# Projected pieces from float32r parts, and values 17 columns wide, in a layer of two causal attentions and a routed network

## The chip, the cores and the metric

The kernel runs on one core of one Trainium2 chip. The metric is the device time of one execution in microseconds (us); the profiled execution also has a span, from its first to its last instruction. Engines are called as in the profile: PE (TensorE; PEld is its weight load), DVE (VectorE), ACT (ScalarE), POOL (GpSimd) and SP (SyncE, which issues the DMAs).

## The reference, cut to what matters

```python
B, T, C = x.shape                       # 32, 512, 256; 16 heads of 16 channels
q, k = split(x @ W_attn + b_attn)       # W_attn 256 x 512
y = causal_attn(q, k, v=x)              # softmax(q k^T / 4) v, per head
e = x[1:] - y[:-1]
k2 = x[:-1] @ W_k2 + b_k2               # W_k2 256 x 256
y2 = causal_attn(q[1:], k2, e)          # with a zero row ahead
a = y @ W_proj + b_proj + y2 @ W_proj + b_proj
x1 = layernorm(x + a)
out = layernorm(x1 + routed)            # routed: 8 experts, two a row, for the 512 rows of batch 0; zero for the rest
```

The router has indices for 512 rows only, those of batch 0. The kernel computes their routed network in the last stretch of its time; for the other batches the second normalization follows the first.

## The kernel before, in words

All five engines run one written-out schedule. Time is a counter: ten slots make a unit, eight units (places 0 to 7) make a batch; there are 32 batches. A unit is one group of four heads of one of the two attentions: places 0 to 3 are the four groups of the first attention, 4 to 7 those of the second. The engines meet by semaphores only, and each works its instructions strictly in the order of the program.

In each slot PE makes a bank of transposed scores (`score_t`, L631) for the unit of now, and a bank of scores (`score`, L642) for the unit five ahead, out of which DVE takes the row maxima (L824). Queries and keys lie in stacks of three float32r parts (high, high, low against high, low, high), so that one pass over 48 to 52 rows gives nearly a float32 product. ACT turns `score_t` into `prob` by exp (L500). There are two `score_t` banks, so PE's slot n waits for the exp of slot n - 2. After every odd slot POOL cuts the triangle of a pair (L422). PE multiplies `prob` by the values in slots 7, 1 and 3 (`weigh`, L592): four heads side by side, each in 32 of the array's columns, with `value[:, kb, head, :]` as stationary operand: 16 channels, a column of ones whose product is the sum of the weights, and 15 more columns of ones that nothing reads. ACT copies all of `out_t` in slot 3 (L524), and PE turns it in slot 5 (L674).

Six pieces a batch project x: `k0` at (place 7, slot 9), `q0` (0, 9), `k1` (1, 9), `q1` (2, 9), `k20` (4, 9), `k21` (5, 9). Each is two float32 products of 128 x 512 into `misc` (L696): the half c = 0 in slot 5, c = 1 in slot 9. A float32 product stands in the trace as two matmul instructions with two weight loads. ACT adds the bias (L518), POOL splits the piece into `part_h` and `part_l` three slots later (L442, L444), and SP copies the parts into the stacks. `x_t` (x turned by the host) has two buffers, loaded two batches ahead.

The normalization of a batch without the routed network is taken twice. The second one, for batches 1 on, lies in place 6 of the batch after: DVE takes statistics in slots 0 to 4, POOL adds epsilon at (6, 5) (`var_eps`, L471), ACT guesses the root at (6, 6) (L260, L262), POOL refines it at (6, 7) in six small operations that end in `shift` (`refine`, L243 to L255), and ACT applies it at (6, 9), (7, 1), (7, 3) and (7, 5) (L267). The first one lies at places 4 and 5 in the same manner.

```python
# POOL, in each time step, in this order:
#   affine_select of the pair (odd slots)   waits s_exp >= time + 1
#   bias add (2, 5); split of a piece, three slots after it
#   slot 0: value2 or y_sum; (4,7) (6,5): var_eps; (4,9) (6,7): refine
# ACT, in each time step:
#   exp; neg_h (7,1) (3,1); piece; slot 3: heads_t; guess_rstd (6,6); apply_norm (6,9) (7,1) (7,3) (7,5)
if now >= KEY_DEPTH:                     # PE, KEY_DEPTH = 2
    e.wait_ge(s_exp, now - KEY_DEPTH + 1)
```

Of the kernel before, what the change touches and what calls it, by code (L numbers as in the profile page):

```python
# [7 lines left out]
F32 = mybir.dt.float32  # L8
F32R = mybir.dt.float32r
# [5 lines left out]
P = 128  # L15
# [49 lines left out]
def build_layer(nc, x, x_turned, w_attn, b_qk, w_k2, w_proj, b_proj,  # L65
# [15 lines left out]
    with ctx:  # L81
# [6 lines left out]
        def sem(name):  # L88
# [3 lines left out]
        wq = sb("wq", [P, halves, 2 * halves, P])  # L92
        wk2 = sb("wk2", [P, halves, halves, P])
# [11 lines left out]
        value1 = sb("value1", [P, blocks, HEADS, 32])  # L105
        value2 = sb("value2", [P, blocks, HEADS, 32])
# [6 lines left out]
        x_t = [sb(f"x_t{i}", [P, halves, tokens]) for i in range(2)]  # L113
# [28 lines left out]
        s_x, s_xt = sem("s_x"), [sem(f"s_xt{i}") for i in range(2)]  # L142
# [3 lines left out]
        s_const, s_ones, s_bias = (sem(f"s_{n}") for n in ("const", "ones", "bias"))  # L146
# [10 lines left out]
        s_mask, s_split, s_value2, s_added, s_biased, s_ln = (  # L157
            sem(f"s_{n}") for n in ("mask", "split", "value2", "added", "biased", "ln"))
# [127 lines left out]
        def _(e):  # L286
            e.dma_start(x_t[0][:, :, :], x_turned[0].rearrange("(h p) t -> p h t", p=P)).then_inc(s_xt[0], 16)
            e.dma_start(wq[:, :, :, :], w_attn.rearrange("(h p) (w n) -> p h w n", p=P, n=P)).then_inc(s_weights, 16)
            e.dma_start(bias_qk[:, :], b_qk).then_inc(s_weights, 16)
            e.dma_start(wk2[:, :, :, :], w_k2.rearrange("(h p) (w n) -> p h w n", p=P, n=P)).then_inc(s_weights, 16)  # L290
# [8 lines left out]
            e.dma_start(x_t[1][:, :, :], x_turned[1].rearrange("(h p) t -> p h t", p=P)).then_inc(s_xt[1], 16)  # L299
# [4 lines left out]
            for time in times:  # L304
# [18 lines left out]
                if (place, slot) == (0, 8) and 2 <= b < batches:  # L323
                    e.wait_ge(s_piece, N_PIECES * (b - 1))
                    e.dma_start(x_t[b % 2][:, :, :], x_turned[b].rearrange("(h p) t -> p h t", p=P)).then_inc(s_xt[b % 2], 16)
# [69 lines left out]
        def _(e):  # L395
# [16 lines left out]
            for time in times:  # L412
# [22 lines left out]
                if piece:  # L435
                    n, i = piece[3], piece[3] % 2
                    e.wait_ge(s_full, n + 1)
                    if n >= 2:

                        was, was_hf = [v[:2] for v in PIECES.values() if v[2] == (n - 2) % N_PIECES][0]  # L440
                        e.wait_ge(s_stack[was, was_hf], 16 * TERMS * SIDES * ((n - 2) // N_PIECES + 1))
                    e.tensor_copy(part_h[i][:, :], part_f[i][:, :]).then_inc(s_split, 1)  # L442
                    e.wait_ge(s_split, 2 * n + 1)
                    e.tensor_tensor(part_l[i][:, :], part_f[i][:, :], part_h[i][:, :].bitcast(F32), ALU.subtract).then_inc(s_split, 1)  # L444

# [133 lines left out]
        def _(e):  # L579
            e.wait_ge(s_const, 11)  # L580

            def weigh(unit, kb, first, count, start=False, stop=False):
# [12 lines left out]

            for time in times:
# [81 lines left out]
                for c in range(halves):  # L678
                    piece = piece_ending(place, slot + 4 * (1 - c), ahead, batches)
                    if piece:  # L680
                        kind, hf, b, n = piece
                        if c == 0:
                            if n == 0:
                                e.wait_ge(s_weights, WEIGHTS)
                            if n % N_PIECES == 0:
                                e.wait_ge(s_xt[b % 2], 16 * (b // 2 + 1))
# [302 lines left out]
```

## Time and profile before

| | |
|---|---|
| median of 3 runs | 2663.38 us (2663.15 to 2669.7) |
| the profiled execution, its time | 2670.42 us |
| its span | 2668.7 us |
| PE busy, DVE, ACT, POOL | 94%, 81%, 69%, 54% |
| mean granted clock of TensorE | 0.976 |

The profiled execution is 7.0 us above the median, and 1.7 us of its time lie outside the span. Busy PE is time in which a matmul is in flight; records of following matmuls overlap, so what a matmul costs is read from the distance between starts or from the chain, not from its duration.

### The profile page before, as it was taken

Reading aid. Unit: us, or ns where it says so; the run is one execution under the profiler, and the core shown is the slowest. Engines: PE = TensorE matmul, PEld = TensorE weight load, DVE = VectorE, ACT = ScalarE, POOL = GpSimd, SP = SyncE. Lnnn points to the kernel's source line nnn. Section 1 sums busy time; section 2 is a strip of 40 time slices with the busy share of each in tenths; the row PEclk is TensorE's granted clock in tenths of the full one; section 3 lists DMA queues with packets and bytes.
Section 4 is the critical chain, followed back from the end, with each engine's and each line's share of the span. In section 5 each row is a group of like instructions: output and inputs, shape, how many; then the busy total and the mean of one; then the engine's idle time right before and its main releaser. Section 6 shows DMA issues by size and latency. Waiting matters only on the chain.

```text
span 2668.7 us, 65100 instructions
## 1 busy us (share of the span) xinstructions
PE 2506.2 (94%) x19286; PEld 1227.1 (46%) x19286; DVE 2166.4 (81%) x9640; ACT 1831.6 (69%) x3574; POOL 1441.9 (54%) x2431
## 2 busy tenths in 40 slices
PE   3999999999999999999999999999999999999897
PEld 1444444444444444444444444444444444444454
DVE  2788888788888888888888888888888888888655
ACT  0477777677777776777777777777777777777653
POOL 2355556556555555655555555555555555555432
PEclk8799999999999999999999999999999999999998
DMA  5455545465555555655455555554555654455211
GB/s 95 87 104 94 93 79 105 91 113 102 104 93 88 93 102 102 113 101 96 91 85 103 99 109 105 105 94 91 86 102 101 114 101 94 87 86 93 63 52 51
DMA packets 187784, 251.23 MB, mean 94 GB/s; under 512 B 26768, under 2 KB 103192, under 8 KB 187416
## 3 DMA queue, kind: packets, MB, share of 16 engines
q1 hardware_dynamic: 187440, 247.07, 50.5%
q8 instruction: 164, 2.69, 0.5%
q14 instruction: 180, 1.47, 0.3%
HBM read 74.60 MB, written 16.78 MB: 34 GB/s over the span
## 4 chain that ended last, share of the span: by engine, by line
PE 77%; DVE 7%; issue 6%; ACT 5%; POOL 3%; SPq 1%; DMA 1%; ACTq 0%; POOLq 0%; DVEq 0%
PE score_t L631 22%; PE out_t L592 21%; PE misc L696 13%; PE score L642 9%; PE misc L731 4%; DVE junk L824 4%; PE turn L674 4%; ACT prob L500 3%; PE score L779 2%; ACT y_t L532 1%; PE misc L718 1%; PE score L795 1%; POOL prob L422 1%; DVE resid L875 1%; DVE max_cols L824 1%
## 5 line engine op out<-in xcount | busy, mean ns | idle before, releaser
L824 DVE CUSTOM_DVE_ANT_0 junk<-score,mask_rows 128x384 bf16<-128x384 f32 (+3 forms) x3584 | 1692.9, 514 | 387.6 <-PE score L642 385.8
L500 ACT ACTIVATE prob<-score_t 128x512 f32<-128x512 f32 x2560 | 1401.5, 596 | 578.3 <-PE score_t L631 573.5
L422 POOL TENSOR_SCALAR_AFFINE_SELECT prob<-prob 128x512 f32<-128x512 f32 (+1 forms) x1280 | 725.9, 568 | 1038.8 <-ACT prob L500 1038.8
L631 PE MATMUL score_t<-stack_q,stack_k 50*128 50x128 f32 (+5 forms) x4096 | 1060.2, 365 | 72.5 <-ACT prob L500 47.6
L642 PE MATMUL score<-stack_k,stack_q 48*128 48x512 f32 (+3 forms) x4096 | 1047.9, 354 | 8.0 <-DMA stack_q<-part_l 5.9
L631 PEld LDWEIGHTS score_t<-stack_q,stack_k 50*128 50x128 f32 (+1 forms) x4096 | 604.1, 186 | 812.7 <-ACT prob L500 689.1
L592 PE MATMUL out_t<-prob,value 128*32 128x512 f32 (+3 forms) x8192 | 719.3, 446 | 0.0
L642 PEld LDWEIGHTS score<-stack_k,stack_q 48*128 48x128 f32 x4096 | 610.8, 189 | 25.4 <-DVE max_cols L824 16.0
L696 PE MATMUL misc<-x_t,wq 128*128 128x512 f32 x512 | 289.5, 650 | 60.9 <-DMA bias<-L_attn_b_proj 31.7
L824 DVE DVE_READ_ACCUMULATOR2_ANT max_cols<- 128x1 f32 x4096 | 338.1, 83 | 0.0
L592 PEld LDWEIGHTS out_t<-prob,value 128*32 128x32 f32 x8192 | 189.0, 109 | 317.2 <-issue 216.0
L444 POOL TENSOR_TENSOR part_l<-part_f,part_h 128x512 fp32r<-128x512 f32 x192 | 245.5, 1279 | 16.4
L518 ACT ACTIVATE part_f<-misc,bias_qk 128x512 f32<-128x512 f32 x192 | 131.9, 687 | 106.1 <-PE misc L696 101.4
L267 ACT ACTIVATE resid<-resid,shift,rstd 128x256 f32<-128x256 f32 x248 | 149.0, 603 | 47.6 <-POOL shift L255 47.6
L674 PE MATMUL turn<-ident,heads_t 128*128 128x128 f32 x1024 | 169.2, 288 | 0.0
L524 ACT ACTIVATE heads_t<-out_t 128x512 f32<-128x512 f32 x256 | 154.2, 602 | 2.2 <-PE out_t L592 2.0
L442 POOL CAST part_h<-part_f 128x512 fp32r<-128x512 f32 x192 | 117.8, 614 | 63.2 <-ACT part_f L518 54.6
L824 DVE CUSTOM_DVE_ANT_0 junk<-score,mask_first 128x128 bf16<-128x128 f32 x512 | 146.3, 286 | 0.0
L696 PE MATMUL misc<-x_t,wk 128*128 128x512 f32 x256 | 141.5, 635 | 0.0
L674 PEld LDWEIGHTS turn<-ident,heads_t 128*128 128x128 f32 x1024 | 108.6, 141 | 47.4 <-ACT heads_t L524 25.3
L731 PE MATMUL misc<-wp,y_t 128*128 128x256 f32 x512 | 127.4, 392 | 0.0
L696 PEld LDWEIGHTS misc<-x_t,wq 128*128 128x128 f32 x512 | 79.6, 195 | 98.9 <-issue 75.4
(83 smaller groups left out, 1380.9 us busy)
## 6 DMA issues: line engine op xcount, KB each, us to landing
stack_k<-part_h SPq DMA_DIRECT2D x512, 128.0 KB, 4.2
stack_k<-part_l SPq DMA_DIRECT2D x256, 128.0 KB, 4.5
stack_q<-part_h SPq DMA_DIRECT2D x256, 128.0 KB, 4.2
x_t<-x_turned SPq DMA_DIRECT2D x32, 512.0 KB, 9.6
x_in<-L_attn_x SPq DMA_DIRECT2D x32, 512.0 KB, 13.4
stack_q<-part_l SPq DMA_DIRECT2D x128, 128.0 KB, 5.1
resid<-L_attn_x SPq DMA_DIRECT2D x32, 512.0 KB, 6.3
layer_out<-resid SPq DMA_DIRECT2D x31, 512.0 KB, 11.6
```

The lines of the kernel that those rows point to most:

```text
L267: e.activation(dst[:, t, :], src[:, t, :], ACT.Identity, bias=shift[:, t:t + 1], scale=rstd[:, 4, t:t + 1]).then_inc(s_apply, 1)
L422: e.affine_select(out=view, in_=view, compare_op=ALU.is_ge, fill=0.0, base=-unit_parts(unit)[1], pattern=[[0, runs], [0, cut], [1, P]], ch ...
L444: e.tensor_tensor(part_l[i][:, :], part_f[i][:, :], part_h[i][:, :].bitcast(F32), ALU.subtract).then_inc(s_split, 1)
L500: e.activation(prob[pair % RING][:, slot % 2 * 512:slot % 2 * 512 + 512], score_t[time % KEY_DEPTH][:, :], ACT.Exp, scale=1.0 / np.sqrt(HE ...
L524: e.activation(heads_t[:, :], out_t[:, :], ACT.Copy).then_inc(s_heads, 1)
L592: done = e.matmul(out_t[32 * h:32 * h + 32, first:first + count], value[:, kb, GROUP * g + h, :], prob[pair % RING][:, at:at + count], sta ...
L631: done = e.matmul(score_t[now % KEY_DEPTH][:, col:col + n], keys[rows, pair, kb * P:(kb + 1) * P], stack_q[b % 2][rows, pair, kb * P:token ...
L642: done = e.matmul(score[number % MAX_DEPTH][:, col:col + n], stack_q[b % 2][rows, pair, qb * P:(qb + 1) * P], keys[rows, pair, 0:n], start ...
L674: done = e.transpose(turn[:, t * P:(t + 1) * P], heads_t[:, t * P:(t + 1) * P], ident[:, :])
L696: done = e.matmul(misc[:, :], w, x_t[b % 2][:, c, :], start=(c == 0), stop=(c == halves - 1))
L731: done = e.matmul(misc[:, j * width:(j + 1) * width], y_t[:, c, t * P:(t + 1) * P], wp[:, c, :], start=(c == 0), stop=(c == halves - 1))
L824: e.tensor_tensor_reduce(junk[count % JUNK][:, 0:n], score[number % MAX_DEPTH][:, col:col + n], mask, 1.0, -3e38, ALU.add, ALU.max, max_co ...
```

## The change

Three things change together. The projections read float32r parts of x turned (`x_t[HIGH]`, `x_t[LOW]`) and of the weights, and do high x high, low weight x high x, and high weight x low x: three one-pass products in place of each float32 one. The weights are split once at the start by DVE; x turned is loaded into one full buffer, `x_full`, and split by POOL at (6, 4) and (6, 7), ahead of the batch's first piece. The values keep 17 of their 32 columns; `out_t` is cleared once, since the rows between the heads are no longer written. The load of x turned for a batch moves behind the split of the batch before it.

```diff
-        wq = sb("wq", [P, halves, 2 * halves, P])
-        wk2 = sb("wk2", [P, halves, halves, P])
+        wq = [sb(f"wq_{part}", [P, halves, 2 * halves, P], F32R) for part in "hl"]
+        wk2 = [sb(f"wk2_{part}", [P, halves, halves, P], F32R) for part in "hl"]
...
-        value1 = sb("value1", [P, blocks, HEADS, 32])
-        value2 = sb("value2", [P, blocks, HEADS, 32])
+        value1 = sb("value1", [P, blocks, HEADS, HEAD_DIM + 1])
+        value2 = sb("value2", [P, blocks, HEADS, HEAD_DIM + 1])
...
# SP
-            e.dma_start(x_t[1][:, :, :], x_turned[1].rearrange("(h p) t -> p h t", p=P)).then_inc(s_xt[1], 16)
...
-                if (place, slot) == (0, 8) and 2 <= b < batches:
-                    e.wait_ge(s_piece, N_PIECES * (b - 1))
-                    e.dma_start(x_t[b % 2][:, :, :], x_turned[b].rearrange("(h p) t -> p h t", p=P)).then_inc(s_xt[b % 2], 16)
+                if (place, slot) == (0, 8) and 1 <= b < batches:
+                    e.wait_ge(s_xsplit, 2 * halves * b)
+                    e.dma_start(x_full[:, :, :], x_turned[b].rearrange("(h p) t -> p h t", p=P)).then_inc(s_xt, 16)
...
# POOL, behind the split of a piece and ahead of slot 0's work, var_eps and refine
+                for c in range(halves):
+                    b = ahead + 2
+                    if (place, slot) == (6, (4, 7)[c]) and 0 <= b < batches:
+                        if c == 0:
+                            e.wait_ge(s_xt, 16 * (b + 1))
+                            if b:
+                                e.wait_ge(s_piece, N_PIECES * b)
+                        e.tensor_copy(x_t[HIGH][:, c, :], x_full[:, c, :]).then_inc(s_xsplit, 1)
+                        e.wait_ge(s_xsplit, 2 * (halves * b + c) + 1)
+                        e.tensor_tensor(x_t[LOW][:, c, :], x_full[:, c, :], x_t[HIGH][:, c, :].bitcast(F32),
+                                        ALU.subtract).then_inc(s_xsplit, 1)
...
# PE
-                    done = e.matmul(out_t[32 * h:32 * h + 32, first:first + count], value[:, kb, GROUP * g + h, :],
+                    done = e.matmul(out_t[32 * h:32 * h + HEAD_DIM + 1, first:first + count], value[:, kb, GROUP * g + h, :],
...
-                        w = wk2[:, c, hf, :] if kind == "k2" else wq[:, c, hf + (0 if kind == "q" else halves), :]
-                        done = e.matmul(misc[:, :], w, x_t[b % 2][:, c, :], start=(c == 0), stop=(c == halves - 1))
+                        for i, (pw, px) in enumerate(zip(PARTS_K, PARTS_Q)):
+                            w = wk2[pw][:, c, hf, :] if kind == "k2" else wq[pw][:, c, hf + (0 if kind == "q" else halves), :]
+                            done = e.matmul(misc[:, :], w, x_t[px][:, c, :], start=(c == 0 and i == 0),
+                                            stop=(c == halves - 1 and i == TERMS - 1))
...
# DVE, at the start
+            e.memset(out_t[:, :], 0.0).then_inc(s_ones, 1)
...
             e.wait_ge(s_weights, WEIGHTS)
+            for i, (parts, full) in enumerate(((wq, wq_full), (wk2, wk2_full))):
+                e.tensor_copy(parts[HIGH][:, :, :, :], full[:, :, :, :]).then_inc(s_wsplit, 1)
+                e.wait_ge(s_wsplit, 2 * i + 1)
+                e.tensor_tensor(parts[LOW][:, :, :, :], full[:, :, :, :], parts[HIGH][:, :, :, :].bitcast(F32),
+                                ALU.subtract).then_inc(s_wsplit, 1)
```

## Rows read from the trace of the kernel before

**Rows 1.** The page, its first part: busy time and share of the span.

```profile
PE 2506.2 (94%) x19286; PEld 1227.1 (46%) x19286; DVE 2166.4 (81%) x9640; ACT 1831.6 (69%) x3574; POOL 1441.9 (54%) x2431
```

**Rows 2.** Weight loads by shape: count, busy us, mean ns, idle before.

```profile
L592 PEld LDWEIGHTS out_t<-prob,value 128*32 128x32 f32 x8192 | 189.0, 109 | 317.2 <-issue 216.0 <-POOL prob L422 100.4
...
L696 PEld LDWEIGHTS misc<-x_t,wq 128*128 128x128 f32 x512 | 79.6, 195 | 98.9 <-issue 75.4 <-ACT part_f L518 7.0
```

**Rows 3.** What PE waited for, 100 to 2500 us: total, times, longest.

```profile
PE score_t L631 <- ACT prob L500: 46.3, 67, 1.0
```

**Rows 4.** Busy time by unit of one batch (window, length, PE, PEld, DVE, ACT, POOL).

```profile
1366.88:1376.57 9.69, 9.14 (x75) 4.12 (x73) 9.42 (x44) 6.89 (x16) 5.46 (x13) 1.00 0.01 3
sum 76.61, PE 73.42 PEld 35.84 DVE 65.32 ACT 56.02 POOL 44.19; mean PE 9.18 PEld 4.48 DVE 8.17 ACT 7.00 POOL 5.52
```

**Rows 5.** The chain that ended last: start, length, what.

```profile
1300.62 0.86 PE misc L696 x2
...
1303.92 1.05 PE misc L696 x2
...
1305.68 1.01 PE out_t L592 x16
```

**Rows 6.** Timeline, PE, one-pass products of 512 columns on the same 64 rows.

```profile
1306.63 0.72 PE L642 MATMUL score<-stack_k,stack_q 48*128 48x512 f32 x2
...
1306.97 0.40 PE L631 MATMUL score_t<-stack_q,stack_k 52*128 52x512 f32 x1
```

**Rows 7.** Timeline, POOL, from slot 2 of place 6.

```profile
1307.14 0.61 POOL L442 CAST part_h<-part_f 128x512 fp32r<-128x512 f32 x1
1307.83 1.28 POOL L444 TENSOR_TENSOR part_l<-part_f,part_h 128x512 fp32r<-128x512 f32 x1
1309.06 0.43 POOL L422 TENSOR_SCALAR_AFFINE_SELECT prob<-prob 128x256 f32<-128x256 f32 x1
...
1310.56 0.23 POOL L471 TENSOR_SCALAR var_eps<-mean_var 128x4 f32<-128x4 f32 x1
1311.82 0.64 POOL L422 TENSOR_SCALAR_AFFINE_SELECT prob<-prob 128x512 f32<-128x512 f32 x1 [1.03 <-ACT prob L500]
...
1313.83 0.23 POOL L255 TENSOR_SCALAR shift<-log_var 128x4 f32<-128x4 f32 x1
```

**Rows 8.** Timeline, ACT, the same stretch.

```profile
1310.82 0.21 ACT L260 ACTIVATE log_var<-var_eps 128x4 f32<-128x4 f32 x1
...
1311.17 0.58 ACT L500 ACTIVATE prob<-score_t 128x512 f32<-128x512 f32 x1
...
1314.09 0.60 ACT L267 ACTIVATE resid<-resid,shift,rstd 128x256 f32<-128x256 f32 x1 [0.65 <-POOL shift L255]
1314.59 1.06 ACT L500 ACTIVATE prob<-score_t 128x512 f32<-128x512 f32 x2
1315.97 0.27 ACT L509 ACTIVATE neg_h<-turn 64x128 fp32r<-64x128 f32 x1 [0.32 <-PE turn L705]
...
1317.59 0.59 ACT L524 ACTIVATE heads_t<-out_t 128x512 f32<-128x512 f32 x1
```

**Rows 9.** Timeline, PE, slots 2 and 5 of place 7.

```profile
1315.87 0.49 PE L631 MATMUL score_t<-stack_q,stack_k 52*128 52x512 f32 x1
...
1318.23 0.66 PE L674 MATMUL turn<-ident,heads_t 128*128 128x128 f32 x4
```

**Rows 10.** Timeline, PE, a long wait near the end of the span.

```profile
2616.61 2.44 PE L795 MATMUL score<-down_w,inner 128*128 128x256 f32 x8 [2.32 <-DVE ffn L934]
```

**Rows 11.** Windows around it; third number from the end: PE's granted clock.

```profile
2618.00:2620.00 2.00, 2.00 (x5) 1.30 (x4) 0.88 (x3) 1.26 (x2) 0.59 (x1) 0.50 0.00 0
2620.00:2622.00 2.00, 2.00 (x4) 0.73 (x4) 0.69 (x1) 0.00 (x0) 0.67 (x1) 0.64 0.48 131
```

**Rows 12.** Timeline, PE, the first piece.

```profile
31.68 3.75 PE L696 MATMUL misc<-x_t,wq 128*128 128x512 f32 x4 [31.68 <-DMA bias<-L_attn_b_proj]
```

**Rows 13.** Timeline, DVE, one copy from SBUF to SBUF.

```profile
1374.94 0.71 DVE L832 COPY value<-x_in 128x1024 f32<-128x1024 f32 x1
```

More of the change, by code:

```diff
@@ L104, in build_layer @@
         ones = nc.alloc_sbuf_tensor_at("ones", [2 * MAX_PARTS, pairs, tokens], F32R, offset=prob_at)
-        value1 = sb("value1", [P, blocks, HEADS, 32])
-        value2 = sb("value2", [P, blocks, HEADS, 32])
+        wq_full = nc.alloc_sbuf_tensor_at("wq_full", [P, halves, 2 * halves, P], F32, offset=prob_at + 4 * pairs * tokens)
+        wk2_full = nc.alloc_sbuf_tensor_at("wk2_full", [P, halves, halves, P], F32, offset=prob_at + 5 * pairs * tokens)
+        value1 = sb("value1", [P, blocks, HEADS, HEAD_DIM + 1])
+        value2 = sb("value2", [P, blocks, HEADS, HEAD_DIM + 1])
         x_in = sb("x_in", [P, blocks, width])
@@ L112, in build_layer @@
         y_t = sb("y_t", [P, halves, tokens])
-        x_t = [sb(f"x_t{i}", [P, halves, tokens]) for i in range(2)]
+        x_full = sb("x_full", [P, halves, tokens])
+        x_t = [sb(f"x_t_{part}", [P, halves, tokens], F32R) for part in "hl"]
         heads_t = sb("heads_t", [P, tokens])
@@ L141, in build_layer @@
         s_weights, s_rows, s_next, s_resid, s_out = (sem(f"s_{n}") for n in ("weights", "rows", "next", "resid", "out"))
-        s_x, s_xt = sem("s_x"), [sem(f"s_xt{i}") for i in range(2)]
+        s_x, s_xt = sem("s_x"), sem("s_xt")
         s_stack = {(kind, hf): sem(f"s_stack_{kind}{hf}") for kind in ("q", "k", "k2") for hf in range(halves)}
         s_maxrow = [sem(f"s_maxrow{i}") for i in range(2)]
-        s_const, s_ones, s_bias = (sem(f"s_{n}") for n in ("const", "ones", "bias"))
+        s_const, s_ones, s_bias, s_wsplit = (sem(f"s_{n}") for n in ("const", "ones", "bias", "wsplit"))
         s_key, s_qry, s_pv, s_turned, s_piece, s_yt_pe, s_proj, s_neg_pe = (
@@ L155, in build_layer @@
             sem(f"s_{n}") for n in ("max", "negl", "value1", "den", "rden", "normal", "attended", "stats", "aggr"))
-        s_mask, s_split, s_value2, s_added, s_biased, s_ln = (
-            sem(f"s_{n}") for n in ("mask", "split", "value2", "added", "biased", "ln"))
+        s_mask, s_split, s_xsplit, s_value2, s_added, s_biased, s_ln = (
+            sem(f"s_{n}") for n in ("mask", "split", "xsplit", "value2", "added", "biased", "ln"))
         s_fin, s_fbias = sem("s_fin"), sem("s_fbias")
@@ L286, in _ @@
         def _(e):
-            e.dma_start(x_t[0][:, :, :], x_turned[0].rearrange("(h p) t -> p h t", p=P)).then_inc(s_xt[0], 16)
-            e.dma_start(wq[:, :, :, :], w_attn.rearrange("(h p) (w n) -> p h w n", p=P, n=P)).then_inc(s_weights, 16)
+            e.dma_start(x_full[:, :, :], x_turned[0].rearrange("(h p) t -> p h t", p=P)).then_inc(s_xt, 16)
+            e.dma_start(wq_full[:, :, :, :], w_attn.rearrange("(h p) (w n) -> p h w n", p=P, n=P)).then_inc(s_weights, 16)
             e.dma_start(bias_qk[:, :], b_qk).then_inc(s_weights, 16)
-            e.dma_start(wk2[:, :, :, :], w_k2.rearrange("(h p) (w n) -> p h w n", p=P, n=P)).then_inc(s_weights, 16)
+            e.dma_start(wk2_full[:, :, :, :], w_k2.rearrange("(h p) (w n) -> p h w n", p=P, n=P)).then_inc(s_weights, 16)
             R, M = SCORE_ROWS, MAX_PARTS
@@ L580, in _ @@
             e.wait_ge(s_const, 11)
+            e.wait_ge(s_ones, 3)
             def weigh(unit, kb, first, count, start=False, stop=False):
@@ L684, in _ @@
                                 e.wait_ge(s_weights, WEIGHTS)
+                                e.wait_ge(s_wsplit, 4)
                             if n % N_PIECES == 0:
-                                e.wait_ge(s_xt[b % 2], 16 * (b // 2 + 1))
+                                e.wait_ge(s_xsplit, 2 * halves * (b + 1))
                             if n:
```

## Prediction

> **What bounds the kernel now.** I read the page first: PE is busy for 94% of the span, DVE for 81%, the others less [rows 1]. A busy PE need not be the bound, so next came the view by unit of one batch in the steady part, 1299.96 to 1376.57 us, cut where PE turns the heads (slot 5): the batch takes 76.6 us, and PE has a matmul in flight in 73.4 of them, DVE works 65.3 [rows 4]. The waits of PE say the same: from 100 to 2500 us it waited 46 us for ACT's exp, in 67 waits of at most 1.0 us [rows 3]. So PE's stream sets the time, and what is taken out of it is gained, where nobody else is close behind. DVE is close in one unit, from slot 5 of place 4 on, with 9.42 of 9.69 us [rows 4]. The last view was the timeline of places 6 and 7, for POOL, ACT and PE [rows 7 to 9]: there the batch's second normalization makes a chain over DVE, POOL and ACT, and ACT's exp, which PE needs two slots later, stands behind it.
>
> **The products.** A float32 product of 512 columns is two instructions. On the chain they take 0.86 us in slot 5 and 1.05 in slot 9 [rows 5]; the 0.19 more in slot 9, where PE comes from products on 64 rows, is the first weight load and the drain, and stays. 0.86 us over 512 columns is four passes of 0.213. For a float32r product over 128 rows there is no row. The nearest is that over 48 and 52 rows: behind the score product begun at 1306.63, with its weight load, the next on the same 64 rows begins 0.34 us later [rows 6], which leaves one pass of 0.21 beside a load of 0.11 to 0.13. So three products take three passes, 0.64, and each pair saves 0.21 us. The loads of the second and third lie under the pass before. Bounds: no less than three passes; no more than two passes for each product, six in all, 0.43 us more than now. I take one, the row shows it. There are 32 x 6 x 2 = 384 such pairs. Those in slot 9 of place 4 (32) save nothing, since PE then waits for DVE, full in that unit; that in slot 5 of place 4 does, as the exps of its unit and with them the first normalization come earlier by as much. The two of place 5 count too: the POOL chain below begins behind the exps and the piece of place 5. 352 x 0.213 = 75 us.
>
> **The values.** The weight load of 32 columns takes 109 ns, that of 128 takes 195 [rows 2]: 0.9 ns a column, 13 ns for 15 columns. Three groups of products a unit, 768 in all, each with one load ahead that nothing covers (four heads load side by side; later ones lie under passes). 768 x 13 ns = 10 us; below, nothing. I take 7, as some groups lie where PE has room. The passes don't change: their length is the columns of `prob`. The rest of what a group pays beyond streaming, 1.01 us less four passes of 0.213, is 0.16 us [rows 5].
>
> **POOL's new work, a wait that appears.** Each batch POOL gets two casts and two subtractions of 128 x 512, the shapes of the split of a piece. There the subtraction begins 0.69 us after the cast, and the next operation 1.23 after that [rows 7]: 1.92 us for a half. On POOL alone, 54% busy, that costs nothing. But it works in order, and behind the first half stand the triangle of slot 5 and `var_eps`, behind the second `refine`. Followed through place 6:
>
> - After the triangle of slot 3 (1309.06, 0.4 us to the next start) the first half runs from 1309.45 to 1311.37. The triangle of slot 5 takes 0.65 more, so `var_eps` begins at 1312.0, not 1310.56: 1.45 late [rows 7].
> - ACT's guess stands in program order ahead of the exp of slot 7, so that exp begins at 1312.6, not 1311.17 [rows 8].
> - The triangle of slot 7 goes from 1311.82 to 1313.27; then the second half, 1.92; then `refine`. `shift` now begins 2.01 after the triangle of slot 7, and will at 1313.27 + 1.92 + 2.01 = 1317.2, 3.37 late [rows 7].
> - ACT's first application waits for it: 1314.09 becomes 1317.46, and the exps of place 7's slots 0 and 1 behind it begin at 1317.96, not 1314.59 [rows 8]. PE's slot 2 waits for the first of them: 1318.5, not 1315.87 [rows 9].
> - ACT gets back the 0.32 us that it waited ahead of `neg_h` [rows 8], so from there it is 3.05 late, with no other gap up to the heads' copy in slot 3: 1317.59 becomes 1320.64, and PE's turn in slot 5 goes from 1318.23 to 1321.28 [rows 8, 9].
>
> From there PE has its own stream to work off, and 3.05 us are lost for good. Both bounds: 3.4 if ACT gets nothing back, 2.5 if PE's slot 2 alone is what is late. What else stands behind: on POOL the triangle of slot 9, wanted in slot 3 of place 7, where PE is late as well; `neg_h` and its DMAs, late with everything else. It happens where a batch has both the second normalization (from batch 1 on) and a later x to split (up to batch 31): in 28 rounds. 28 x 3.05 = 85 us.
>
> **What the stall does to PE's clock.** From about 1315.9 (the end of the weighing and a turn) to 1318.5 PE then does nothing, 2.6 us, and little in the 3 us before. In the steady part the clock is 1.00 with waits of at most 1.0 us [rows 3, 4]. Near the end PE waited 2.32 us [rows 10], and 1.4 us after that wait the clock fell to 0.50, for 2 us and for 0.72 of the next window (at 0.64 in the mean): 3.4 us at 1.2 GHz [rows 11]. Such a stretch does 1.7 us less work; some 0.4 of it lies where PE waits for ACT anyway. So 1.3 us each time. Bounds: never, or after each of 28 stalls (36 us). I take three of five, as the new wait is a little longer than the one that was followed by a fall: 28 x 0.6 x 1.3 = 22 us.
>
> **The start.** DVE splits 1024 and 512 columns of weights ahead of the first piece. A copy of 1024 columns takes 0.71 us [rows 13]; by bounds of once and twice that for the larger cast and subtraction and half for the smaller, 2.1 to 4.3 us, I take 3.1. The first piece, at half clock, took 3.75 us for two float32 products, eight passes of 0.43 and a load [rows 12]; with six single passes of 0.43 it takes 2.6, and two pieces lie ahead of the first scores: 2.2 less. One 512 KB load leaves the start: about 1 less. Together nothing.
>
> **The sum.** 85 - 75 - 7 + 0 + 22 = 25 us more, against the profiled execution's 2670.4 us (span 2668.7, 1.7 around it): 2695. That execution was 7.0 above the median, so against 2663.4 I say 2688.
>
> **One rule weighed.** By the Trainium skill, "TensorE: Matmul & The Clock Gate", section "Weight-path perf modes", weights of 128 columns whose type is not float32 load by a faster way, measured there at about twice the speed. The float32r loads of this trace are of 128 columns, and their load in the 0.34 us of [rows 6] shows none of it. By the rule each product group in slot 9 would save half of its first load of about 0.11 us, 192 x 0.055 = 11 us; by the row, nothing, and the sum goes by the row.
>
> **The rivals.**
> 1. *The stall without the clock's fall.* For it: PE still does some work in the 3 us before the gap. Then 25 - 22 = 3 us more: 2666, between 2652 and 2678.
> 2. *The narrow values pay for more than a load (the other side).* If all of the 0.16 us that a group costs beyond its passes goes by the width of the weights, 15/32 of it, 0.075 us, is saved in each of 768 groups: 58 us instead of 7. With the stall and no fall of the clock: 2666 - 51 = 2615; with the fall 2637. It decides from 21 ns a group on (16 us, twice the bound for a change that shows). Against it: most of that 0.16 should be the way through the array and its drain, which have nothing to do with width.
> 3. *The products load faster.* If a float32r load of 128 columns takes 0.055 us less than the 0.11 of [rows 6], the 192 groups in slot 9 save 11 us: 2677. This is what the rule above would do here.
> 4. *A float32r product over 128 rows is two passes.* 352 x 0.64 = 225 us more than in the sum: 2913. Against it: [rows 6].
> 5. *The clock stays down for longer after each stall.* If two such stretches follow each stall, 28 x 2 x 1.5 = 84 in place of 22: 2750.
>
> **How the numbers follow.** My forecast (stall and fall) 0.45, with its own range 2674 to 2704; rival 1 0.23; rival 2 0.15; rival 3 0.06; rival 4 0.02; rival 5 0.09. What a measurement can tell from no change is 0.3%, 8 us: 2655 to 2671. Slower: all of the forecast but little, rivals 3 to 5, a quarter of rival 1: 0.63. The same: most of rival 1: 0.17. Faster: rival 2 and the low end of rival 1: 0.20. The range 2630 to 2718 leaves out rivals 4 and 5 and the lower half of rival 2, under 2 in 10.
>
> **What would show it.** Right: ACT's wait for `shift` in place 6 of about 3.3 us where it is 0.65 now; PE's waits for the exp up by some 70 to 90 us; in the chain more POOL and ACT; product groups of three at 0.64 us in slot 5; windows at 0.5 clock behind the stalls. Wrong: no new wait of ACT; three products over 0.7 us; value groups shorter by more than 0.03 us; a batch period away from the places' stall that shrinks by less than 2 us. The prediction fails most easily in the balance of two terms near 80 us, in which an error of 10% in one is the 0.3% that can be told.

## The result, and the profile after

The changed kernel takes 2752.24 us (median of 4 runs, 2748.9 to 2754.43) against 2663.27: 1.0328 times as long, with an interval of 1.0307 to 1.0349. I had forecast 2688, slower, with a range that ends at 2718. The direction was right, the size was not: 89 us in place of 25.

The page of the changed kernel, the line that answers to [rows 1]:

```profile
PE 2524.4 (92%) x19670; PEld 1323.2 (48%) x19670; DVE 2174.3 (79%) x9645; ACT 1829.0 (66%) x3574; POOL 1557.0 (57%) x2559
```

PE is busy for 18 us more, and its share falls. So the time did not go into PE's work alone: waits came in. The waits of the changed kernel, 100 to 2600 us (total, times, longest), to be set beside [rows 3]:

```profile
ACT resid L270 <- POOL shift L258: 110.1, 58, 3.1
PE score_t L647 <- ACT prob L515: 109.1, 127, 2.5
ACT log_var L263 <- POOL var_eps L486: 41.1, 28, 1.7
```

The last row is the count that the prediction needed: 28 rounds in which ACT waits for `var_eps`. PE's wait for the exp is 63 us above the 46.3 of [rows 3], which end at 2500 us. One round, POOL's timeline (start, length, what; it answers to [rows 7]):

```profile
1349.37 0.41 POOL L424 TENSOR_SCALAR_AFFINE_SELECT prob<-prob 128x256 f32<-128x256 f32 x1
1349.74 0.60 POOL L456 CAST x_t_h<-x_full 128x512 fp32r<-128x512 f32 x1
1350.43 1.28 POOL L458 TENSOR_TENSOR x_t_l<-x_full,x_t_h 128x512 fp32r<-128x512 f32 x1
...
1352.38 0.23 POOL L486 TENSOR_SCALAR var_eps<-mean_var 128x4 f32<-128x4 f32 x1
1353.64 0.64 POOL L424 TENSOR_SCALAR_AFFINE_SELECT prob<-prob 128x512 f32<-128x512 f32 x1 [1.03 <-ACT prob L515]
1354.23 0.61 POOL L456 CAST x_t_h<-x_full 128x512 fp32r<-128x512 f32 x1
1354.93 1.29 POOL L458 TENSOR_TENSOR x_t_l<-x_full,x_t_h 128x512 fp32r<-128x512 f32 x1
...
1357.59 0.23 POOL L258 TENSOR_SCALAR shift<-log_var 128x4 f32<-128x4 f32 x1
```

From the triangle of slot 7 (1353.64) to `shift` (1357.59) it is 3.95 us; in [rows 7] it was 2.01. ACT in the same stretch (it answers to [rows 8]), then PE (to [rows 9]):

```profile
1352.64 0.20 ACT L263 ACTIVATE log_var<-var_eps 128x4 f32<-128x4 f32 x1 [1.68 <-POOL var_eps L486]
...
1357.85 0.60 ACT L270 ACTIVATE resid<-resid,shift,rstd 128x256 f32<-128x256 f32 x1 [3.09 <-POOL shift L258]
1358.36 1.06 ACT L515 ACTIVATE prob<-score_t 128x512 f32<-128x512 f32 x2
```

```profile
1356.22 0.30 PE L724 MATMUL turn<-ident,max_cols 128*64 128x128 f32 x1
1358.98 0.50 PE L647 MATMUL score_t<-stack_q,stack_k 52*128 52x512 f32 x1 [2.46 <-ACT prob L515]
...
1362.46 1.12 PE L690 MATMUL turn<-ident,heads_t 128*128 128x128 f32 x4
```

The rows show the chain of the prediction: `shift` late, the exp behind it late, PE idle for 2.46 us. The last row belongs to the term that I had undersized. The turn of four blocks takes 1.12 us where [rows 9] has 0.66: PE now works at 1.2 GHz. Windows over the same stretch (third number from the end: the granted clock):

```profile
1356.00:1358.00 2.00, 0.52 (x13) 0.12 (x3) 0.27 (x2) 0.15 (x1) 1.58 (x8) 1.00 0.03 3
1358.00:1360.00 2.00, 1.02 (x4) 0.39 (x4) 0.45 (x1) 2.00 (x6) 1.52 (x3) 0.90 0.00 0
1360.00:1362.00 2.00, 2.00 (x17) 1.06 (x16) 1.05 (x5) 1.79 (x5) 0.41 (x1) 0.50 0.04 8
1362.00:1364.00 2.00, 2.00 (x10) 1.57 (x9) 1.49 (x8) 1.78 (x4) 0.64 (x1) 0.50 0.14 29
1364.00:1366.00 2.00, 2.00 (x11) 1.17 (x9) 0.24 (x1) 0.21 (x1) 0.01 (x1) 0.50 0.45 94
1366.00:1368.00 2.00, 2.00 (x20) 0.78 (x17) 1.93 (x12) 1.03 (x3) 0.64 (x1) 0.89 0.35 119
```

The clock is down for 6.8 us here. By windows of 1 us over the whole span, the changed kernel has 28 stretches at half clock between 300 and 2520 us, one in each of the 28 rounds: 20 of 6.8 us, 7 of 10.2 and one of 3.4, 212 us together. The kernel before has nine in the same part of the span, 41 us, each 1.0 to 2.2 us behind a wait of 1.0 us for the exp.

A round of the changed kernel has two waits of PE: one of 0.9 us, which the kernel before has as well (1.0 there), and about 5 us later the long one. In 21 rounds the fall comes in the long wait or at most 2.1 us after it, as above. In the 7 rounds with 10.2 us it comes before the long wait, 1.2 to 2.5 us behind the short one, and lasts through the long one, of which 1.2 to 2.3 us are left, as PE, slow by then, comes to it later. One of these rounds, PE's two waits and one window between them:

```profile
951.83 0.38 PE L647 MATMUL score_t<-stack_q,stack_k 52*128 52x256 f32 x1 [0.89 <-ACT prob L515]
...
957.18 0.79 PE L647 MATMUL score_t<-stack_q,stack_k 52*128 52x512 f32 x1 [1.47 <-ACT prob L515]
```

```profile
954.00:955.00 1.00, 1.00 (x16) 0.34 (x8) 0.66 (x4) 0.00 (x0) 0.83 (x4) 0.50 0.33 41
```

The products and values, in the chain of waits that ended last (they answer to [rows 5]) and in the weight loads (to [rows 2]; count, busy us, mean ns):

```profile
1373.33 0.70 PE misc L714 x3
...
1376.45 0.89 PE misc L714 x3
...
1378.23 0.99 PE out_t L608 x16
```

```profile
L608 PEld LDWEIGHTS out_t<-prob,value 128*17 128x17 f32 x8192 | 163.3, 97 | 317.2 <-issue 197.2 <-POOL prob L424 119.7
...
L714 PEld LDWEIGHTS misc<-x_t_h,wq_h 128*128 128x128 f32 x256 | 53.2, 208 | 96.4 <-issue 75.1 <-ACT part_f L533 4.5
```

Three float32r products take 0.70 us in slot 5 and 0.89 in slot 9, against 0.86 and 1.05: 0.16 less, not 0.21. The group over the values takes 0.99 for 1.01.

### The profile page after: what moved, and what is told of

The parts are those of the page before. It is cut to its first block, busy times and chain, and to the rows that moved or that the text cites. A ratio compares the mean times of both kernels' runs of the same rounds, so it can differ in the third digit from the quotient of the medians.

```text
span 2752.2 us, 66033 instructions
## 1 busy us (share of the span) xinstructions
PE 2524.4 (92%) x19670; PEld 1323.2 (48%) x19670; DVE 2174.3 (79%) x9645; ACT 1829.0 (66%) x3574; POOL 1557.0 (57%) x2559
## 4 chain that ended last, share of the span: by engine, by line
PE 63%; POOL 13%; ACT 10%; issue 9%; DVE 4%; SPq 1%; DMA 1%; ACTq 0%; POOLq 0%; DVEq 0%
PE score_t L647 18%; PE out_t L608 16%; PE misc L714 10%; PE score L658 7%; ACT prob L515 6%; PE misc L750 4%; POOL prob L424 4%; PE turn L690 3%; POOL x_t_l L458 3%; DVE junk L849 2%; PE score L798 1%; ACT y_t L547 1%; PE misc L737 1%; ACT resid L270 1%; POOL x_t_h L456 1%
## 5 line engine op out<-in xcount | busy, mean ns | idle before, releaser
L647 PE MATMUL score_t<-stack_q,stack_k 50*128 50x128 f32 (+5 forms) x4096 | 1116.6, 377 | 131.2 <-ACT prob L515 109.4
L658 PE MATMUL score<-stack_k,stack_q 48*128 48x512 f32 (+3 forms) x4096 | 1101.4, 364 | 11.5 <-DMA stack_q<-part_l 9.4
L647 PEld LDWEIGHTS score_t<-stack_q,stack_k 50*128 50x128 f32 (+1 forms) x4096 | 634.8, 192 | 781.9 <-ACT prob L515 611.5
L608 PE MATMUL out_t<-prob,value 128*17 128x512 f32 (+3 forms) x8192 | 723.3, 449 | 0.0
L658 PEld LDWEIGHTS score<-stack_k,stack_q 48*128 48x128 f32 x4096 | 641.8, 194 | 24.2 <-DVE max_cols L849 12.6
L608 PEld LDWEIGHTS out_t<-prob,value 128*17 128x17 f32 x8192 | 163.3, 97 | 317.2 <-issue 197.2
L714 PE MATMUL misc<-x_t_h,wq_h 128*128 128x512 f32 x256 | 135.5, 529 | 63.9 <-DVE wk_l L830 34.6
L444 POOL CAST part_h<-part_f 128x512 fp32r<-128x512 f32 x192 | 131.1, 683 | 62.8 <-ACT part_f L533 51.9
L714 PE MATMUL misc<-x_t_l,wq_h 128*128 128x512 f32 x256 | 110.0, 430 | 0.0
L714 PE MATMUL misc<-x_t_h,wq_l 128*128 128x512 f32 x256 | 109.6, 428 | 0.0
```

The costliest lines, as they stand in the source:

```text
L608: done = e.matmul(out_t[32 * h:32 * h + HEAD_DIM + 1, first:first + count], value[:, kb, GROUP * g + h, :], prob[pair % RING][:, at:at + c ...
L647: done = e.matmul(score_t[now % KEY_DEPTH][:, col:col + n], keys[rows, pair, kb * P:(kb + 1) * P], stack_q[b % 2][rows, pair, kb * P:token ...
L658: done = e.matmul(score[number % MAX_DEPTH][:, col:col + n], stack_q[b % 2][rows, pair, qb * P:(qb + 1) * P], keys[rows, pair, 0:n], start ...
L714: done = e.matmul(misc[:, :], w, x_t[px][:, c, :], start=(c == 0 and i == 0), stop=(c == halves - 1 and i == TERMS - 1))
```

## The experiments

The runs are compared by their times and by one table from the traces: the time from one turn of the heads (slot 5) to the next, in us by place, as a median over the 28 batches that have a stall in the changed kernel. "1-2" is the time from the turn in place 1 to that in place 2, "6-0" that from place 6 to place 0 of the next batch. The last column is the time at half clock between 120 and 2600 us. None of it is a single row: it is worked out from the starts of the four-block turns and from the granted clock. The kernel before was timed again beside each series of runs and took 2663.3 to 2666.9 us, so a difference between two series carries some 3 us.

```
kernel                  1-2    2-4    4-5    5-6    6-0    0-1    batch   half clock
before                  9.90   20.59  9.72   8.88   18.27  9.25   76.61    51
values only             9.85   20.56  9.71   8.86   18.26  9.22   76.46    65
behind normalization    9.53   20.26  9.55   8.71   18.09  9.07   75.21    31
wait filled             9.53   20.26  9.51   8.71   21.01  9.07   78.09    48
after                   9.54   20.24  9.53   8.71   23.37  9.07   80.46   212
first half only         9.53   20.25  9.57   8.71   19.37  9.07   76.50    85
splits alone            9.85   20.56  9.68   8.86   23.73  9.21   81.89   283
six in slot 5          10.23   20.95 10.24   9.42   19.88  9.77   80.49    96
one product             9.07   21.72  9.46   8.39   17.78  8.59   75.01    82
one product, late bias  9.08   19.78  9.46   8.39   17.78  8.59   73.08   112
```

**Values only.** The kernel before with nothing but the values 17 wide:

```diff
-        value1 = sb("value1", [P, blocks, HEADS, 32])
-        value2 = sb("value2", [P, blocks, HEADS, 32])
+        value1 = sb("value1", [P, blocks, HEADS, HEAD_DIM + 1])
+        value2 = sb("value2", [P, blocks, HEADS, HEAD_DIM + 1])
...
-                    done = e.matmul(out_t[32 * h:32 * h + 32, first:first + count], value[:, kb, GROUP * g + h, :],
+                    done = e.matmul(out_t[32 * h:32 * h + HEAD_DIM + 1, first:first + count], value[:, kb, GROUP * g + h, :],
```

> The kernel before with only the values cut to 17 columns (and the one clearing of out_t that goes with it); projections, x and weights as before. If the narrow weight load is worth what its 12 ns say (97 against 109 ns, 768 groups), the time falls by up to 9 us: 2654 to 2663. If the narrow values are part of the 89 us, through another way of loading or a slower product, it rises by 20 us or more. If the whole fixed part of a group went by the width, it falls to about 2615.

Measured: 2667.11 us against 2666.86, ratio 0.9997 (0.9984 to 1.001). By the table a batch is 0.15 us shorter, 5 us in all, and the time doesn't show even that. My second rival, that narrow values pay for more than a load, is out.

**No splits in the steady part.** The changed kernel, where GpSimd splits only the first x:

```diff
-                    if (place, slot) == (6, (4, 7)[c]) and 0 <= b < batches:
+                    if (place, slot) == (6, (4, 7)[c]) and b == 0:
```

> The changed kernel in which POOL splits x for batch 0 only; the later splits are left out, so every batch is projected from batch 0's x. Theory A (POOL's splits delay the second normalization, and all of the loss is the stall behind it and the halved clock after it): the rest of the change is a gain, 2663 - 75 - 7 = about 2580, 2565 to 2600, and no episodes of half clock beyond those of the kernel before. Rival B (the products, the values or the loads cost time themselves): 2640 or more.

Measured: 2619.56 us, ratio 0.9818 (0.9802 to 0.9834). The stall and its clock are worth 133 us (2752.24 less 2619.56), but the gain left is 47 us, not 82: the products save less than I had said. This was the first sign of an error on each side of the sum.

**The wait filled.** The changed kernel with nine products of 512 columns on PE inside the wait, written to a bank that is overwritten later. The stall of everybody else stays; only PE's idleness goes:

```diff
+                if (place, slot) == (7, 1) and 2 <= ahead <= batches - 3:
+                    for _ in range(FILL):
+                        e.matmul(misc[:, :], wq[HIGH][:, 0, 0, :], x_t[HIGH][:, 0, :], start=True, stop=True)
```

> The changed kernel with nine products of 128x512 put on PE into the wait at slot 1 of place 7, of batches that split x; nobody reads their output, and they fit in the 2.5 us in which PE waits for the exp. Theory A1 (what costs most is not the wait but the clock that is halved after it, 6.8 us in most batches): the stalls stay and the time falls by 60 to 80 us, to 2675 to 2695, and the mean granted clock goes back from 0.947 to 0.97 or more. Rival A2 (the wait costs by itself, the clock is a mark of it only): 2752 within 10 us, or more by the added work.

Measured: 2701.82 us, ratio 1.0127 (1.0108 to 1.0146), 50 us less than the changed kernel, with 9 x 28 products more. PE's timeline in one round, and the windows around it:

```profile
1331.81 2.33 PE L730 MATMUL misc<-x_t_h,wq_h 128*128 128x512 f32 x9
...
1334.49 0.50 PE L648 MATMUL score_t<-stack_q,stack_k 52*128 52x512 f32 x1 [0.34 <-ACT prob L516]
```

```profile
1335.00:1337.00 2.00, 1.93 (x18) 0.89 (x18) 1.78 (x6) 2.00 (x6) 0.81 (x2) 1.00 0.04 8
1337.00:1339.00 2.00, 2.00 (x18) 1.47 (x15) 1.24 (x9) 1.96 (x6) 0.48 (x1) 1.00 0.09 21
```

The score product still waits for its exp, and in this round the clock behind it stays at 2.4 GHz. No round has a fall behind the filled wait. In 13 of the 28 the clock falls ahead of it all the same, 1.3 to 2.2 us behind the short wait of 0.9 us, and for 3.4 us each time. Summed over all batches, the way from place 6 to 0 is 82 us longer than without the stall (the next run), and in the changed kernel, where the long wait is empty, a further 55. The times say the same: 84 us for the stall (2701.82 less 2618.27), 50 for the clock (2752.24 less 2701.82). The 84 still hold a few us of clock, 48 us at half against 31. The 50 us belong to 164 us more at half clock: one us at half clock costs about a third of a us here.

**The splits behind the normalization.** The changed kernel with the two halves at place 6, slot 7, behind `refine`, and place 7, slot 2; each half of a piece's products waits for its own half of x:

```diff
-                    if (place, slot) == (6, (4, 7)[c]) and 0 <= b < batches:
+                    if (place, slot) == ((6, 7), (7, 2))[c] and 0 <= b < batches:
```

> The changed kernel with the same splits of x, but issued on POOL behind the normalization: the first half after refine at (6, 7), the second at (7, 2), and each product waits for its half only. All work is kept. Theory A: the place of the splits and not their amount costs the time; ACT's wait for shift goes back to about 0.7 us, and the time is near that of the kernel without splits, 2575 to 2605. Rival C (POOL has no room for 3.8 us more a batch wherever they lie, since the triangles behind them come late): 2640 or more.

Measured: 2618.27 us, ratio 0.9817 (0.9798 to 0.9836). It leaves nothing out, and it is faster than both kernels, by 1.8% than the one before: the work on POOL costs nothing that shows once nothing urgent stands behind it. Its waits, 100 to 2600 us:

```profile
ACT resid L270 <- POOL shift L258: 45.9, 59, 2.8
PE score_t L648 <- ACT prob L516: 43.3, 69, 1.0
```

Both are back at about what they were ([rows 3]). The time is that of the run without splits, within 1.3 us. What I had expected, some 2580, was missed by the same 38 us in both, which is the products' term.

**One half in the way.** The changed kernel with the first half left at place 6, slot 4, and the second at place 7, slot 2:

```diff
-                    if (place, slot) == (6, (4, 7)[c]) and 0 <= b < batches:
+                    if (place, slot) == ((6, 4), (7, 2))[c] and 0 <= b < batches:
```

> The changed kernel with the first half of the split where the change puts it (place 6, slot 4) and only the second moved behind the normalization (place 7, slot 2). GpSimd then reaches var_eps some 1.4 us late and the shift as much, instead of 1.45 and 3.37. Theory, that a stall costs what it lasts beyond some 0.3 us of cover and that the clock falls only behind a long one: 28 x 1.1 = 31 us above 2618, 2650 us, and fewer than ten stretches at half clock in the steady part. Rival, that every stall at this place brings a stretch at half clock: 31 + 50 = 81 us above, 2700 us, with a stretch behind each of the 28.

Measured: 2659.72 us, ratio 0.9976 (0.9958 to 0.9994), 41 us above the version behind the normalization; both of my figures, 31 and 81, miss it, the first by less. The waits:

```profile
ACT resid L270 <- POOL shift L258: 56.9, 58, 1.2
ACT log_var L263 <- POOL var_eps L486: 41.3, 29, 1.7
```

In the rounds without half clock the way from place 6 to 0 is 0.94 us longer (19.03 for 18.09), 26 us for 28 rounds; over all rounds it is 39 us longer. From 300 us on there are 17 stretches at half clock where the version behind the normalization has 6, 54 us more. So the short stall costs its length and sometimes the clock; only the rounds with the long one have a fall every time.

**The splits alone.** The kernel before with the values 17 wide, float32 products as ever, and GpSimd's four operations at the places of the change, written to tiles that nobody reads:

```diff
+                    if (place, slot) == (6, (4, 7)[c]) and 1 <= b < batches:
...
+                        e.tensor_copy(spare_h[:, :], x_t[b % 2][:, c, :]).then_inc(s_spare, 1)
+                        e.wait_ge(s_spare, k + 1)
+                        e.tensor_tensor(spare_l[:, :], x_t[b % 2][:, c, :], spare_h[:, :].bitcast(F32),
+                                        ALU.subtract).then_inc(s_spare, 1)
```

> The kernel before with the values 17 wide, and GpSimd's four split operations of the change at place 6, slots 4 and 7, for batches 1 to 29, written to spare tiles that nobody reads; the products stay full float32 ones. Theory, that the stall and the clock behind it belong to the place of the splits and have nothing to do with the products: 29 x 3 us of stall and some 50 us of clock on 2667, 2800 us, and a stretch at half clock behind each. Rival, that the clock's fall needs the float32r products (a TensorE that had been less busy before the wait): 2751 us, with few such stretches.

Measured: 2799.15 us, ratio 1.0514 (1.0499 to 1.053), with a stretch at half clock in each of the 28 rounds, here of 10.2 us in 27 of them. These 27 don't stand behind the long wait: they begin ahead of it, 1.3 to 1.9 us behind the short wait, which is mostly 1.06 us here, and last through it. PE's short wait in one round, and the window in which the clock is down first:

```profile
1293.16 0.38 PE L648 MATMUL score_t<-stack_q,stack_k 52*128 52x256 f32 x1 [1.06 <-ACT prob L516]
```

```profile
1295.00:1296.00 1.00, 1.00 (x12) 0.24 (x8) 0.96 (x4) 0.00 (x0) 0.92 (x3) 0.50 0.73 84
```

The splits cost 132 us on top of the values-only kernel, and the changed kernel has 134 on top of its version without the stall. So the loss doesn't need the float32r products, and the two parts of the change add up. Where in the round the clock falls, and for how long, isn't the same in the two kernels; why isn't shown.

**Six products in slot 5.** The version behind the normalization, with the three products of slot 5 done twice, the first time as a closed group whose result is overwritten:

```diff
-                        for i, (pw, px) in enumerate(zip(PARTS_K, PARTS_Q)):
+                        for extra, i, pw, px in [(more, i, *part) for more in ((True, False) if c == 0 else (False,))
+                                                 for i, part in enumerate(zip(PARTS_K, PARTS_Q))]:
```

> The kernel with the splits behind the normalization (2618.27 us), with the three products of slot 5 done twice (the first time as a closed group of their own, whose result is overwritten): 192 more trios, nothing else. If three float32r passes cost 3 x 0.23 = 0.69 us on the path, 132 us more, 2750 us; if they cost what I took in the prediction, 3 x 0.213 = 0.64, 123 us more, 2741 us. If half of it vanishes in waits that PE has anyway for exponentials or for VectorE, 2684 us; this would say that the saving of the products was lost in the same way.

Measured: 2765.83 us, ratio 1.0367 (1.0328 to 1.0406), 148 us more. Away from the clock each of the six trios of a batch takes 0.69 to 0.71 (9.53 to 10.23, 20.26 to 20.95, and so on; in place 6 to 0 the rounds without half clock take 18.8): 4.2 us a batch, 135 us. In the chain:

```profile
1301.99 1.41 PE misc L718 x6
...
1305.82 0.90 PE misc L718 x3
```

So a pass of 512 float32r columns is 0.235 us, and in slot 5 all of it lies on the path that sets the time. The other 13 us fit the clock (65 us more at half), and the four runs of this kernel lie between 2750 and 2775.

**One product.** The version behind the normalization with two of the three terms left out:

```diff
-                        for i, (pw, px) in enumerate(zip(PARTS_K, PARTS_Q)):
+                        for i, (pw, px) in enumerate([(HIGH, HIGH)]):
```

> The kernel with the splits behind the normalization (2618.27 us), each group of three float32r products cut to its first, high part times high part: two of the three terms of a projected piece are left out. 768 products of 512 columns go, of 0.23 us each by the pitch in the trace: 177 us of TensorE. Theory, that TensorE's own time sets the end in slot 5 but that in slot 9 the next group of scores waits for an exponential anyway: the 384 in slot 5 give 88 us, those in slot 9 between nothing and half of theirs, so 2480 to 2530 us, and the waits of PE for ACT grow. Rival, that TensorE is the bound everywhere: 2441 us. Rival, that VectorE's and ScalarE's waits take it all: 2600 us or more.

Measured: 2625.33 us, ratio 0.9877 (0.9838 to 0.9916). 177 us of PE's work taken out, and the kernel is 7 us slower than with it. It looks like proof that PE isn't the bound. The table says otherwise: every place got shorter but those from 2 to 4, which got 1.5 us longer in the median and 1.9 in the mean. POOL and then PE in place 2:

```profile
1324.45 0.64 POOL L424 TENSOR_SCALAR_AFFINE_SELECT prob<-prob 128x512 f32<-128x512 f32 x1 [1.29 <-ACT prob L516]
1328.26 2.35 POOL L432 TENSOR_TENSOR resid<-resid,bias 128x1024 f32<-128x1024 f32 x1 [3.17 <-DMA resid<-L_attn_x]
1330.56 1.27 POOL L424 TENSOR_SCALAR_AFFINE_SELECT prob<-prob 128x512 f32<-128x512 f32 x2
```

```profile
1331.25 1.66 PE L609 MATMUL out_t<-prob,value 128*17 128x384 f32 x12 [1.99 <-POOL prob L424]
```

With a faster PE, POOL comes to its bias add before the residual's load has landed, waits 3.17 us with two triangles behind it, and PE waits for those. This is the rule and no single case: from 100 to 2600 us POOL waits for that load 28 times, 67 us in all, and PE 27 times for such triangles, 36 us.

**One product, the bias add later.** The same with that add moved from place 2, slot 5 to slot 9:

```diff
-                if (place, slot) == (2, 5) and 0 <= ahead - 1 < batches:
+                if (place, slot) == (2, 9) and 0 <= ahead - 1 < batches:
```

> The kernel with one product for three (2625.33 us; two of three terms left out), with GpSimd's bias add to the second residual moved from place 2, slot 5 to slot 9 of the same place, so that it no longer waits 3.2 us for its load in front of a mask. Theory: that wait hid the worth of the products. By the turns of the trace the places away from it were 0.46 us shorter (two) or 0.32 (two), so with it gone a batch is some 2.6 us shorter than with three products: 2618 less 80 to 90 us, 2530 to 2545 us. Rival: the wait only took slack that was there, TensorE isn't what bounds the batch, and the time stays above 2600.

Measured: 2567.5 us, ratio 0.9629 (0.9602 to 0.9656). The stall is gone (19.78 in place of 21.72), and 58 us with it. A batch is 2.13 us shorter than with three products: 0.45 to 0.48 in 1-2, 2-4 and 0-1, 0.32 in 5-6, 0.31 in 6-0, 0.09 in 4-5. Of twelve groups that lost two passes, the equal of about four and a half shows. That is 68 us over the batches; 51 were measured. The clock takes the rest as far as it can be told (112 us at half, 31 with three products). Where the other seven and a half groups go isn't shown; PE's waits for DVE's row maxima grow from 92 to 189, by 28 us.

**The bias add later, three products.** The same edit on the version behind the normalization.

> The kernel with the splits behind the normalization (2618.27 us), with the same bias add moved to slot 9. There it waited for its load 8.9 us in all, 11 times. Theory: 5 to 10 us less, 2608 to 2613 us. Rival: it was hidden, 2618 us. Both kernels stand below the one before by about 1.8 to 2.1%.

Measured: 2617.54 us, ratio 0.9822 (0.9791 to 0.9853): no gain. With three products POOL waits for that load 11 times, 8.9 us in all, and what it waits there is hidden.

## Why the prediction was right in direction and wrong in size

The direction was right; two steps of the prediction failed. One is how long the clock stays down ("3.4 us", "three of five"): 50 us where I had 22. The other is the price of a float32r pass, together with how many of the products' places give the gain: 49 us where I had 75, or 82 with the values. The sum by the runs: 2667 with the values, less 49 for the products, 84 for the stall, 50 for the clock: 2752. It closes by construction, since each term is the difference of two kernels that differ in it; what stands beside it as a check are the places of the trace (82 us and 55) and the splits alone (132 us).

- *The stall, 85 us predicted:* 84, or 82 by the places of the trace. ACT's wait for `shift` is 3.09 (I had said about 3.3), `log_var` waits in exactly 28 rounds, PE's slot 2 waits 2.46. The walk through the instruction order of POOL, ACT and PE was right at each step that the rows show. The term itself is shown by the filled wait, where little but the stall is left.
- *The clock, 22 us predicted:* 50. This is the step "I take three of five", with "1.3 us each time". The clock fell in all 28 rounds, for 6.8 or 10.2 us in 27 of them, not for the 3.4 of [rows 11]. That is 1.8 us a round. It is the mechanism of my fifth rival, to which I gave 0.09. That one had 84 us: it was right on the length and wrong on the price, 1.5 us for 3.4 at half clock, where the runs have about a third of it, some 1.1. Its 2750 comes so near to the time by luck, as the products' error makes up for that. I had one example of a wait in front of a fall, and took its length for that of all. The premise was wrong too: I wrote that in the steady part the clock is 1.00 with waits of at most 1.0 us, from the windows of one batch. The same trace has nine falls behind such waits between 300 and 2520 us, and in 7 of the 28 rounds of the changed kernel it is such a wait that the fall follows.
- *The products, 75 us predicted:* about 49. Two errors of size. First, [rows 6] has 0.34 us from one product's start to the next with a load between, and I read it as a 0.21 pass beside a load of 0.11 to 0.13. The pass is 0.235 and the load about 0.11; six products of one stationary shape in a row give it. Three passes of 0.235 are 0.70, so a pair saves 0.16, not 0.213: 56 us for 352 pairs. The prediction had named 0.64 as what would show it right and "over 0.7 us" as what would show it wrong; 0.70 and 0.71 stand at that mark. Second, I let all products of slot 9 but those of place 4 count. In the table the saving from the values-only kernel to the one behind the normalization is 0.32, 0.30, 0.16, 0.15, 0.17 and 0.15 us: eight groups of twelve. In most places only one of the two is gained. Part of the other may go into PE's waits for DVE, 64 waits of 19.4 us in all in the values-only kernel and 92 of 24.1 in the one behind the normalization. That is 5 us of the 20 (four groups, 0.16, 32 batches); where the rest goes stays open. 8 x 0.16 x 32 is 41 us; the batch shows 1.25, 40 us; the rest of the 49 fits the clock, 31 us at half in place of 65.
- *The values, 7 us predicted:* nothing that the time shows, 5 by the trace.
- *The start, nothing predicted:* 1.9 us more up to the first turn of row maxima (89.21 for 87.36). The first piece starts 2.9 us later, behind DVE's split of the weights, for which I had said 3.1:

```profile
34.62 0.77 PE L714 MATMUL misc<-x_t_h,wq_h 128*128 128x512 f32 x1 [34.62 <-DVE wk_l L830]
35.19 0.63 PE L714 MATMUL misc<-x_t_h,wq_l 128*128 128x512 f32 x1
35.61 0.63 PE L714 MATMUL misc<-x_t_l,wq_h 128*128 128x512 f32 x1
```

- *The rule weighed:* the Trainium skill, "TensorE: Matmul & The Clock Gate", section "Weight-path perf modes", has weights of 128 columns that are not float32 load faster. The trace doesn't agree for float32r: the loads of `L714` take 208 ns in the mean, in a kernel with more time at half clock, and 191 to 197 in the version behind the normalization, where the float32 ones of [rows 2] took 195; and slot 9 costs 0.19 us more than slot 5 as it did with float32 (0.89 less 0.70, 1.05 less 0.86).

So the terms were wrong by 33 us (products and values, 82 for 49) and by 28 (clock), both toward faster; the other 3 us of the 64 are what the kernel before took more beside these runs. The clock's bound was 36 us, since I bounded how often it falls and not for how long; the pass of 0.21 had as its next bound six passes, and no error of its own in reading one row. The range had to miss when both were off.

## What to carry to other kernels

Before work is put on a lightly loaded engine that works in order, ask what stands behind it there: four operations of 3.8 us a batch cost 134 us in front of a normalization's scalars, and nothing that shows 3 to 5 slots later. A new wait of the tensor engine should be priced with the clock that goes with it, which here cost more than half as much as the wait of 2.5 us itself; and the falls in the trace at hand, behind its shorter waits too, should be counted first. And when work taken from the bounding engine gives nothing back, look by stage for one new wait (a load that was in time only because the kernel was slow) before you call the engine unimportant.

## What the runs showed that I had not expected

- Between 300 and 2520 us the stretches at half clock come in lengths of 3.4, 6.8 and 10.2 us, with one of 13.7 among all. With less work on PE there are more of them even without a long stall: 6 with three products, 21 with one (both from 120 to 2600 us).
- The kernel with nine useless products in each long wait is 50 us faster than without: no fall follows the filled wait.
- In the first pieces passes of 512 columns begin 0.43 us apart (35.19 and 35.61 above), twice the 0.235 of later, while the windows there show a granted clock of 1.00:

```profile
34.00:36.00 2.00, 1.38 (x3) 1.16 (x4) 0.70 (x2) 0.00 (x0) 0.00 (x0) 1.00 0.00 0
```

- The view misleads there for longer in some executions. For the kernels before and after, and the late bias add, it shows 54.6 to 64.9 us at half clock that end between 106 and 114 us. For the wait filled and the version behind the normalization it shows none of that, as if the start had been at full clock. But the clock's record of the latter has its first entry at 104.7 us, and PE's passes up to there are as slow as in the others, 0.43 us apart:

```profile
91.62 0.63 PE L717 MATMUL misc<-x_t_h,wq_l 128*128 128x512 f32 x1
92.05 0.63 PE L717 MATMUL misc<-x_t_l,wq_h 128*128 128x512 f32 x1
```

```profile
90.00:92.00 2.00, 2.00 (x6) 1.39 (x6) 2.00 (x10) 0.00 (x0) 0.00 (x0) 1.00 0.15 23
```

  From 105.9 us on they are 0.23 apart. So the mean granted clocks of two executions can differ by 0.01 with nothing behind it, and the table above leaves the first 120 us out. What the start really differs by is small: the first turn of the heads comes at 110.67 us there and at 114.87 in the changed kernel.
- PE's work isn't symmetric here: 135 us added in slot 5 cost all of it, and of 177 us taken out in slots 5 and 9 together about 68 showed in the batches.
